# Expert lists, turned rows, weight splits and centred down rows moved ahead by some steps around the first expert

## The reference

```python
x = x + _layernorm(_L0_attn_ref(_layernorm(x), w_qkv, w_proj, b_proj))
x = x + _layernorm(_L0_ffn_ref(_layernorm(x), gate_w, Wg, Wu, Wd, Sg, Su, Sd))
```

```python
scores = softmax(flat_x @ gate_w.T).T                  # 16 x 8192
topk_weight, topk_idx = lax.top_k(scores, 1024)        # per expert
xg = flat_x[topk_idx]
h  = gelu(xg @ Wg.T) * (xg @ Wu.T)                     # 1024 x 1024 per expert
eo = (h @ Wd.T) * topk_weight[..., None]
out = zeros.at[topk_idx].add(eo) + (gelu(x @ Sg.T) * (x @ Su.T)) @ Sd.T   # shared part, 512 wide
```

## Time and profile before

| | us |
|---|---|
| median of 3 runs | 1985.97 |
| lowest and highest | 1985.50, 1986.74 |
| the profiled execution | 1984.56 |
| its span, first to last instruction | 1982.8 |

### The profile page before, as it was taken

One profiled execution on the slowest core, in us unless ns is written; L12 is line 12 of the kernel. 1 busy time (PEld: TensorE's weight loads), 2 busy tenths in 40 slices (PEclk: granted clock), 3 DMA queues, 4 the chain that ended last, 5 costly groups with the idle time before them and its releaser, 6 DMA issues.

```text
span 1982.8 us, 29127 instructions
## 1 busy us (share of the span) xinstructions
PE 1948.3 (98%) x10638; PEld 1654.4 (83%) x10638; DVE 1366.1 (69%) x2601; ACT 1036.0 (52%) x1929; POOL 525.9 (27%) x627
## 2 busy tenths in 40 slices
PE   8999999999999999999999999999999999999997
PEld 7888888888878888788888888888888888888886
DVE  6777787778776777667676666657565656666647
ACT  5456576666655434445454454545454555445445
POOL 0032032123120001222431332343234323332246
PEclk9999999999999999999999999999999999999999
DMA  3113324233243111333434434343435344434566
GB/s 128 54 33 108 75 98 115 88 115 99 73 154 133 60 64 52 119 79 93 100 84 104 91 91 86 90 102 90 104 89 103 85 108 92 100 81 101 152 218 171
DMA packets 153338, 197.38 MB, mean 100 GB/s; under 512 B 104448, under 2 KB 121088, under 8 KB 145152
## 3 DMA queue, kind: packets, MB, share of 16 engines
q1 hardware_dynamic: 127824, 158.00, 25.5%
q0 software_dynamic: 25392, 37.77, 12.0%
HBM read 114.38 MB, written 59.34 MB: 88 GB/s over the span
## 4 chain that ended last, share of the span: by engine, by line
PE 64%; DVE 3%; POOL 1%; issue 1%; ACT 1%; DVEq 0%; DMA 0%; SPq 0%; ACTq 0%; POOLq 0%
PE mo_psD L1620 12%; PE mo_psG L60 7%; PE mo_psU L60 7%; PE mo_psU L62 7%; PE mo_psU L61 7%; PE mo_psG L62 7%; PE mo_psG L61 7%; PE mo_psD L1622 6%; PE mo_psD L60 1%; PE mo_psD L62 1%; PE mo_psD L61 1%; PE mo_psX L1345 1%; DVE mo_F L1934 1%; POOL mo_H_lo L2261 0%; DVE mo_HF L1950 0%
## 5 line engine op out<-in xcount | busy, mean ns | idle before, releaser
L1746 ACT ACTIVATE mo_HF<-mo_psG 128x512 f32<-128x512 f32 x320 | 191.3, 598 | 407.7 <-PE mo_psU L62 322.2
L1950 DVE TENSOR_TENSOR mo_HF<-mo_psU,mo_HF 128x512 f32<-128x512 f32 x320 | 220.5, 689 | 223.8 <-ACT mo_HF L1746 213.1
L2243 POOL DMA_INDIRECT ACC<-OUT,mo_GI x128 | 201.8, 1577 | 643.2 <-DVE OUT L2036 631.4
L1620 PE MATMUL mo_psD<-wd,mo_H_hi 128*128 128x512 f32 x1024 | 360.8, 393 | 0.2 <-DVE OUT L2036 0.2
L1622 PE MATMUL mo_psD<-wd,mo_H_lo 128*128 128x256 f32 x1024 | 289.3, 283 | 0.0
L60 PE MATMUL mo_psG<-mo_XT_hi,wg_hi 128*128 128x512 f32 x640 | 255.9, 400 | 3.9 <-DVE mo_HF L1950 1.9
L60 PE MATMUL mo_psU<-mo_XT_hi,wu_hi 128*128 128x512 f32 x640 | 253.6, 396 | 0.0
L62 PE MATMUL mo_psG<-mo_XT_hi,wg_lo 128*128 128x512 f32 x640 | 252.6, 395 | 0.0
L62 PE MATMUL mo_psU<-mo_XT_hi,wu_lo 128*128 128x512 f32 x640 | 252.6, 395 | 0.0
L61 PE MATMUL mo_psG<-mo_XT_lo,wg_hi 128*128 128x512 f32 x640 | 252.4, 394 | 0.0
L61 PE MATMUL mo_psU<-mo_XT_lo,wu_hi 128*128 128x512 f32 x640 | 252.3, 394 | 0.0
(11 more groups left out here) (355 smaller groups left out, 4152.7 us busy)
## 6 DMA issues: line engine op xcount, KB each, us to landing
X1a<-wg_in SPq DMA_DIRECT2D x16, 1024.0 KB, 4.9
X1a<-wu_in SPq DMA_DIRECT2D x16, 1024.0 KB, 4.8
X1a<-wd_in SPq DMA_DIRECT2D x16, 1024.0 KB, 4.8
XN<-XG SPq DMA_DIRECT2D x8, 1088.0 KB, 4.2
X<-x_in SPq DMA_DIRECT2D x8, 1024.0 KB, 5.4
out_dram<-X SPq DMA_DIRECT2D x8, 1024.0 KB, 6.4
XN2T<-xn2T SPq DMA_DIRECT2D x8, 1024.0 KB, 5.1
X1a<-xt_in SPq DMA_DIRECT2D x7, 1024.0 KB
```

Of the source, the lines that this page charges most:

```text
L1620: pe.matmul(psD[:, t % 2, :], h_hi, wd_both[:, it, :, :].rearrange("p z d -> p (z d)"), start=(it == 0), stop=False)
L1746: a.activation(HF[:, it % 2, :], psG[:, it % 2, :], ACT.Gelu).then_inc(s_gelu, 1)
L1950: v.tensor_tensor(HF[:, it % 2, :], psU[:, it % 2, :], HF[:, it % 2, :], ALU.mult).then_inc(s_mul, 1)
L2243: g.indirect_dma_start(out=io["ACC"], out_offset=bass.IndirectOffsetOnAxis(ap=GI[n % 2][:, 4 * tb + t:4 * tb + t + 1], axis=0), in_=OUT[:, ...
```

## The change

In the last shared blocks some work is issued at other places of the engines' orders. (1) A new method `vector_first` issues `v_acc(1)`, `v_dec(0)` (step 43) and `v_acc(3)`, `v_dec(1)` (step 46) on DVE ahead of the wait for that step's GELU. (2) PE's `turn` stands ahead of all twelve matmuls of step 47 instead of in their middle. (3) ACT's two `x_hi` stand ahead of its wait for step 46, DVE's two `x_lo` ahead of the product of step 46. (4) The six `w_lo` of expert 0 move from `down(11)` to step 46 (quarter 1, ahead of `vector_first`), step 47 (quarter 2) and step 48 (quarter 3). (5) Expert 0's two `sum_rows` and two `center` move from steps 50 to 52 to DVE's `down(11)`, ahead of the product of step 50. No instruction is added or dropped.

```diff
--- before.py
+++ after.py
@@ -1151,8 +1151,6 @@
             self.v_lo1(v, 1)
             self.v_hival(v, 1)
         if x == 35:
-            self.v_acc(v, 1)
-            self.v_dec(v, 0)
             self.v_lo1(v, 2)
         if x == 36:
             self.v_hival(v, 2)
@@ -1160,6 +1158,12 @@
             self.v_acc(v, 2)
             self.v_lo1(v, 3)
             self.v_hival(v, 3)
+
+    def vector_first(self, v, x):
+
+        if x == 35:
+            self.v_acc(v, 1)
+            self.v_dec(v, 0)
         if x == 38:
             self.v_acc(v, 3)
             self.v_dec(v, 1)
@@ -1573,10 +1577,10 @@
                             topk.sum(pe, s - 2 - SHIFT)
                         topk.tensor_at(pe, s - 0.25 - SHIFT)
                         tail.p_middle(pe, s)
-                        if b == E0 - 1 and it == 3:
-                            for dk in range(KD):
-                                turn(E0, dk)
-
+
+                if b == E0 - 1 and it == 3:
+                    for dk in range(KD):
+                        turn(E0, dk)
                 if is_b(b):
                     up(it, XT[b % 2], (bsw["g"], bsw["u"]), middle)
                     topk.tensor_at(pe, s - SHIFT)
@@ -1740,6 +1744,9 @@
 
             def step(b, it):
                 s = base[b] + it
+                if is_b(b) and s - SHIFT == 38:
+                    x_hi(E0, 0)
+                    x_hi(E0, 1)
                 wait(a, s_up, s + 1)
                 if s >= 2:
                     wait_lo(a, *before(b, it, 2))
@@ -1755,9 +1762,6 @@
                     if 34 <= x < 38:
                         w_hi("g", 0, x - 34)
                         w_hi("u", 0, x - 34)
-                    if x == 38:
-                        x_hi(E0, 0)
-                        x_hi(E0, 1)
                 elif is_e(b):
                     if it < 2 and E0 + BY_PE <= b + 1 < D0:
                         split_rows(b + 1, it)
@@ -1944,8 +1948,19 @@
                 if t + 4 == n:
                     i.then_inc(s_o, 1)
 
+            def gate_up_lo(quarter):
+                for w in "gu":
+                    w_lo(w, 0, quarter)
+
             def step(b, it):
                 s = base[b] + it
+                if is_b(b):
+                    if s - SHIFT == 38:
+                        gate_up_lo(1)
+                    topk.vector_first(v, s - SHIFT)
+                    if s - SHIFT == 38:
+                        x_lo(E0, 0)
+                        x_lo(E0, 1)
                 wait(v, s_gelu, s + 1)
                 v.tensor_tensor(HF[:, it % 2, :], psU[:, it % 2, :], HF[:, it % 2, :], ALU.mult).then_inc(s_mul, 1)
                 if s and (b < D0 or (b, it) == (D0, 0)):
@@ -1958,19 +1973,17 @@
                     topk.vector_at(v, x)
                     if x in (36, 37):
                         w_lo("gu"[x - 36], 0, 0)
-                    if x == 38:
-                        x_lo(E0, 0)
-                        x_lo(E0, 1)
+                    if x == 39:
+                        gate_up_lo(2)
                 elif is_e(b):
+                    if (b, it) == (E0, 0):
+                        gate_up_lo(3)
                     if (b, it) == (E0, 2):
                         scores_of(0)
                     n, tb = expert(b)
                     if tb == 0 and n and it < 2:
                         sum_rows(n, it)
-                    if b == E0 and it == 2:
-                        sum_rows(0, 0)
-                        sum_rows(0, 1)
-                    if tb == 0 and it in (3, 4):
+                    if tb == 0 and n and it in (3, 4):
                         center(n, it - 3)
                     task = weight_task(b, it)
                     if task:
@@ -2022,9 +2035,10 @@
                     if b < E0 - 1:
                         topk.vector_at(v, base[b + 1] + 1.5 - SHIFT)
                     else:
-                        for quarter in range(1, 4):
-                            for w in "gu":
-                                w_lo(w, 0, quarter)
+                        for half in range(2):
+                            sum_rows(0, half)
+                        for half in range(2):
+                            center(0, half)
                 if is_e(b):
                     n, tb = expert(b)
                     for t in range(4):
```

## The result

The changed kernel took 1989.86 us (median of 17 runs, 1987.62 to 1991.90) against 1986.64 us (median of 17 runs, 1984.82 to 1988.08) for the kernel before: ratio 1.0014, 95% interval 1.0007 to 1.0020, or 2.8 us (1.4 to 4.0) more by the ratio and 3.2 by the medians. The profiled execution took 1988.27 us with a span of 1986.5 us; before it was 1984.56 and 1982.8.

What follows compares the result with a forecast made beforehand. The prediction took PE, with work for 98% of the span, as the bound. It summed -3.6 (gain before step 48), +4.5 (net stall at step 52) and +2.0 (clock) to +2.9 us, 1988.9 us, range 1985.0 to 1992.0.

Steps and rivals of the forecast that it cites:

- the likeliest case: PE stalls in front of step 52 and the clock falls: +2.9 us, 1988.9 us, chance 0.50.
- the gain in front of step 48: Earlier lists, turn and split let PE start step 48 sooner, by 3.1 to 4.1 us, taken as 3.6.
- the clock: Granted clock at its lower level, 1.2 GHz, when step 52 starts; cost 0 to 3.2 us, taken as 2.0.
- Lists sooner by 3.4 us: `v_acc(1)` starts at about 775.1, and the `LIST` stores, `IDX` load and POOL's copy move 3.4 us sooner with it.
- Gathers: Before `turn`, the fourth gather is issued by 789.3 and lands about 2 us later; gathers stretched once or twice, not four times.
- the rival of late gathers: Gathers landing late idle PE at `turn`: 2.2 us of the gain lost, +5.1 us, 1991.1 us, chance 0.12.
- the bound: Late-gather limit in front of `turn`: all four gathers stretched to 2.39 us, issued by 793.6 and landed by 795.6.
- the 797.0 to 798.1: Sign to look for: the time in us at which step 48's first matmul should start in the changed kernel.
- Splits at nothing: The six `w_lo`, moved to steps 46 to 48, fit into DVE's free time and are costed at nothing.
- Wait of 6.4 us at step 52: PE stands still 6.4 us before step 52, whose product queues behind sums and centrings awaiting the down weights.
- 1.9 us back at steps 52 to 55: Small waits for products that the centring passes had pushed back go, returning 1.9 us.
- Sum: Total over the kernel: -3.6 + 4.5 + 2.0 = +2.9 us, a forecast of 1988.9 us.

Runs made afterwards that it cites:

- f2: The kernel before, run again without any edit, for a second profile on another chip; step 46 to 48 took 9.46 us.
- f4: Changed kernel with sums and centrings at their old place and the six weight splits back in `down(11)`; ratio 0.9992 to the kernel before.
- e1: Changed kernel with expert 0's two sums and two centrings put back to steps 50 to 52; 1980.20 us against 1982.50 for the kernel before, ratio 0.9991.
- e2: Kernel before with only the two sums and two centrings moved into `down(11)`, ahead of the product of step 50; 1989.02 us against 1982.50, ratio 1.0035.
- e4: Changed kernel with expert 0's down-weight load issued ahead of block 11's store; 1979.42 us against 1982.50 for the kernel before, ratio 0.9983.
- e3: Changed kernel with 26 unused matmuls added on PE in its wait for step 52; ratio 1.0019 to the kernel before.
- The timed pair: Changed kernel with 26 unused matmuls added in PE's wait for step 52, against the changed kernel, on one chip; 1986.56 against 1987.24 us.
- f1: Changed kernel again without any edit, on another chip, with a second profile; ratio 1.0025 to the kernel before.
- g1: Changed kernel a third time without any edit, on another chip; 1987.24 us, ratio 1.0024 to the kernel before.
- g3: Changed kernel with 13 unused matmuls added in PE's wait for step 52; 1987.48 us, ratio 1.0022 to the kernel before.
- g4: Changed kernel with the down-weight load ahead of block 11's store, run again on another chip; 1978.30 us against 1982.94 for the kernel before, ratio 0.9978.

## Why the prediction came out right

The time lies 1.0 us from the forecast and the likeliest case is the one that happened, but two terms were off and offset each other in the profiled pair: the gain in front of step 48 (2.8 us for 3.6) and the clock (1.3 us for 2.0).

- *Lists sooner by 3.4 us:* right. `v_acc(1)` at 775.08 (forecast 775.1), POOL's copy at 780.61 (781.3).
- *Gathers:* the fourth was issued by 789.55 (forecast 789.3), and `turn` was held by `v_acc(3)` and not by its rows, so the rival of late gathers did not happen. All four were stretched, to 1.26 to 2.24 us. From the page "SBUF — State Buffer" of the Trainium skill I had read one or two; whether they waited or ran slower the trace doesn't tell. None took the 2.39 us of the bound, so the sum stood.
- *Gain in front of step 48, forecast 3.6 us:* 2.8 us in the profiled pair (11.99 to 9.18; step 48 at 798.27, just outside the 797.0 to 798.1) but 1.7 us in every undelayed profile. The side of the new kernel was right: 797.05 - 789.15 = 7.9 us forecast from step 46 to 48, 7.75 measured without the delay. I saw the 2.06 us between transposes and copy and doubted it for the new kernel only. The failed step is that I took 801.14 as the start of step 48 to gain from. In that profile 2.5 of the 12.0 us between steps 46 and 48 are a delay that f2, the same program, doesn't have.
- *Splits at nothing:* right within the interval of f4 (0.9983 to 1.0001 against 0.9983 to 1.0000 in e1).
- *Wait of 6.4 us at step 52:* right, 12.52 - 5.95 = 6.6 us, with the chain as forecast: `sum_rows` 6.99 us after the end of `down(11)` (6.9), the product of step 50 right behind `center`. e1 and e2 show that this edit alone makes it, e4 that the load's place in SP's queue was the cause.
- *1.9 us back at steps 52 to 55:* right. With the clock kept up they take 8.9 us, 1.7 to 1.8 less than before (e3, e4).
- *Clock, 2.0 us:* the mechanism is shown by e3. The size in the profiles is 10.23, 11.62 and 11.02 less 8.9, so 1.3, 2.7 and 2.1 us. The timed pair gives 0.7 by the medians and 1.6 to 1.7 group by group.
- *Sum:* forecast +2.9. Measured +2.8 in the first comparison and +5.0 and +4.8 in f1 and g1, all by the ratios. From undelayed profiles it is -1.7 + 6.6 - 1.8 + 2.0 = +5.1. So the close hit owes something to luck: without the delay the gain is 1.9 us smaller than forecast and the sum beyond 4 us. If the runs of the first comparison had the delay, as both of their profiles do, that would explain their smaller number, since it is 2.5 us in the kernel before and 1.4 in the changed one. The medians point that way: the kernel before took 3.7 to 4.1 us more there than on the other chips, the changed kernel 2.4 to 2.6. For timed runs it was not shown.

## What to carry to other kernels

Work that waits for a DMA may stand ahead of a product on an in-order engine only if the DMA is surely there; move the load ahead in its own queue first, then the work. Look in the queue of the load for what it stands behind: here a store that it had nothing to do with. And before a stretch of one profile is costed, ask whether its lags are the usual ones for their kind; a second profile of the kernel before, on another chip, showed that 2.5 us of the stretch are not always there. When two variants are compared, look also whether their times fall into groups: here a median moved by the share of runs in each group as much as by the edit.

## What was not expected of the hardware

- PE's signals came late in one stretch in two of the fourteen profiles, as far as the modelled ends of matmuls tell. In the kernel before the GELU of step 46 started 1.2 us behind the end of its matmuls, and ACT's copy 2.06 us behind the start of `turn` where f2 has 0.66. In the changed kernel `v_acc(3)` started at 794.08 though chunk 3's matmuls (from 790.56, 1.20 us) ended at 791.8, and the copy 1.12 us behind `turn` where g1 has 0.63. In the others the first of each follows at once. The cause is open; POOL was issuing gathers in all of them.
- The granted clock fell 2.5 (changed), 3.2 (e2), 5.0 (f1), 4.4 (g1) and 3.3 us (g3) after PE's last matmul, 2.2 us in the earlier trace rows, and in step 52 between 6 and all 12 matmuls ran at the lower level. At it a 128x512 float32 matmul follows the one before by 0.43 us instead of 0.23, and its record is 0.63 us long instead of 0.39: the price of a matmul is the 0.20 us of spacing.
- The clock also fell around a wait of 2.18 us near 566 us, in five of fourteen profiles, and each time after PE had begun again (in f2 PE at 567.08 and the clock at about 567.2, in g4 at 567.40 and about 568.8). Two waits of about 2 us near 795 and 800 us in the kernel before left it at 1.00.
